# Decoder layer on one core: reloads of the turned x spread over one step, and one copy turned into a maximum

## The reference

```
x = x + self_attention(layernorm(x))      # 32 query heads, 16 key/value heads of 32, causal softmax
x = x + cross_attention(layernorm(x))     # 64 context positions per batch, 8 key/value heads
x = x + ffn(layernorm(x))                 # Wd @ (silu(Wg x) * (Wu x)), 3584 wide, 4-bit weights
```

## Time and profile before

| | |
|---|---|
| median of 3 runs | 2796.19 us (2792.77 to 2798.71) |
| profiled execution, its own time | 2796.21 us |
| its span in the profile | 2794.3 us |
| PE busy | 2581.9 us, 92% of the span |
| DVE busy | 2054.9 us, 74% |
| ACT busy | 1572.4 us, 56% |
| POOL busy | 1235.5 us, 44% |
| DMA, mean | 73 GB/s |

### The profile page before, as it was taken

The page is one execution under the profiler, slowest core; times in us unless marked ns, Lnnn a source line. Parts: engine busy times, 40 slices in busy tenths (PEclk is TensorE's granted clock), DMA queues, the critical chain, the costliest instruction groups (busy, mean ns, idle before and its releaser), DMA issues.

```text
span 2794.3 us, 52658 instructions
## 1 busy us (share of the span) xinstructions
PE 2581.9 (92%) x18536; PEld 1397.0 (50%) x18536; DVE 2054.9 (74%) x2844; ACT 1572.4 (56%) x2794; POOL 1235.5 (44%) x1068
## 2 busy tenths in 40 slices
PE   5889999999974359899999999999999999999999
PEld 3567767667663234344444444444444444444444
DVE  4656768767775768787787869788787868778773
ACT  3456666656663468474655647465564747465550
POOL 2356667767774424252433424243433425243330
PEclk9999999999987669999999999999999999999999
DMA  5243433333222321111111112121111212111112
GB/s 192 91 132 100 121 114 120 102 111 100 81 73 59 128 80 56 51 61 38 60 49 50 53 45 60 38 68 38 53 52 45 61 38 66 40 60 46 52 34 120
DMA packets 153268, 205.34 MB, mean 73 GB/s; under 512 B 34160, under 2 KB 85872, under 8 KB 153072
## 3 DMA queue, kind: packets, MB, share of 16 engines
q1 hardware_dynamic: 153072, 202.97, 23.0%
HBM read 157.16 MB, written 44.04 MB: 72 GB/s over the span
## 4 chain that ended last, share of the span: by engine, by line
PE 60%; DVE 2%; issue 1%; ACT 1%; DMA 1%; POOL 0%; SPq 0%; DVEq 0%; ACTq 0%; POOLq 0%
PE f_bank L1501 39%; PE f_down L1521 21%; DVE line L1625 1%; DMA codes<-in_codes 1%; DVE f_stats L1639 0%; DVE fT_l L1652 0%; ACT f_xn L1561 0%; ACT line L1550 0%; ACT fT_h L1569 0%; PE f_down L1483 0%; DVE w L1631 0%; ACT line L1547 0%; DVE h L1661 0%; DVE y L1666 0%; DVE f_mean_var L1642 0%
## 5 line engine op out<-in xcount | busy, mean ns | idle before, releaser
L1625 DVE TENSOR_TENSOR line<-line 128x512 f32<-128x512 f32 x1008 | 919.4, 962 | 46.7 <-issue 30.9
L1550 ACT ACTIVATE line<-codes 128x512 f32<-128x512 int32 x1008 | 591.2, 620 | 382.6 <-DVE line L1625 284.8
L1501 PE MATMUL f_bank<-fT_h,up_h 128*128 128x512 f16 x1792 | 680.2, 380 | 3.7 <-DVE fT_l L1652 2.4
L1501 PE MATMUL f_bank<-fT_l,up_h 128*128 128x512 f16 x1792 | 680.2, 380 | 0.0
L1501 PE MATMUL f_bank<-fT_h,up_l 128*128 128x512 f16 x1792 | 680.2, 380 | 0.0
L532 POOL TENSOR_TENSOR p_l<-p,p_h 128x512 f16<-128x512 f32 x320 | 369.9, 1164 | 243.0 <-ACT p_h L945 242.6
L1666 DVE SCALAR_TENSOR_TENSOR y<-f_down,y 128x1024 f32<-128x1024 f32 x224 | 274.2, 1224 | 190.7 <-PE f_down L1521 190.7
L1431 POOL TENSOR_TENSOR up_l<-w,up_h 128x512 f16<-128x512 f32 x112 | 145.8, 1301 | 529.2 <-ACT up_h L1555 529.2
L1426 POOL TENSOR_TENSOR w<-w,scales 128x512 f32<-128x512 f32 x168 | 263.8, 1570 | 227.7 <-DVE w L1631 227.7
L1115 DVE TENSOR_REDUCE block_max<-bank 128x4 f32<-128x512 f32 x320 | 218.8, 686 | 195.3 <-PE bank L704 193.0
L1521 PE MATMUL f_down<-dn_h,hT_h 128*128 128x512 f16 x896 | 340.6, 380 | 9.0 <-DVE y L1666 9.0
(11 more groups left out here) (157 smaller groups left out, 4245.4 us busy)
## 6 DMA issues: line engine op xcount, KB each, us to landing
codes<-in_codes SPq DMA_DIRECT2D x168, 256.0 KB, 3.0
scales<-in_scales SPq DMA_DIRECT2D x336, 128.0 KB, 2.9
nat_parts<-nat SPq DMA_DIRECT2D x48, 256.0 KB, 2.0
q_rows<-nat_parts SPq DMA_DIRECT2D x96, 128.0 KB, 2.7
x_unit<-in_x SPq DMA_DIRECT2D x64, 128.0 KB, 2.7
x<-x_unit SPq DMA_DIRECT2D x64, 128.0 KB, 2.3
y<-x SPq DMA_DIRECT2D x4, 2048.0 KB, 12.3
out<-y SPq DMA_DIRECT2D x16, 512.0 KB, 2.6
```

The costliest lines, as they stand in the source:

```text
L1501: mm = nc.tensor.matmul(bank[(GATE, UP)[kind] + n % 2][:, :], w[:, chunk, kind, P * c:P * c + P], x[:, c, cols], start=(m == 0), stop=(m = ...
L1550: op = nc.scalar.activation(line[:, m, :], codes[:, slot, :], ACT.Copy, scale=slope, bias=intercept)
L1625: nc.vector.tensor_tensor(line[:, n + 2, :], line[:, n, :], line[:, n + 2, :], ALU.max)\
```

## The change

`load_turned` takes the part's number i and issues one reload. The four calls move from the head of SP's step i = 10 into step i = 9, between that step's other transfers. The waits of each reload are the same as before: `turned_stored`, and then `x_used` for parts 0 to 2 and `proj_done` for part 3. The third of `row_maxima`'s four instructions becomes a reduction by maximum over an axis of length one.

```diff
-            def load_turned(b):
+            def load_turned(b, i):
                 sp.wait_ge(turned_stored, 16 * TURNED_BY[b])
-                for i in range(QT):
-                    if i < QT - 1:
-                        sp.wait_ge(x_used, (QT - 1) * (b - 1) + i + 1)
-                    else:
-                        sp.wait_ge(proj_done, NP * b)
-                    sp.dma_start(xT[:, i, :, :, :]..., dram["xT"][b % 2, i, :, :]).then_inc(turned_loaded[i], 16)
+                if i < QT - 1:
+                    sp.wait_ge(x_used, (QT - 1) * (b - 1) + i + 1)
+                else:
+                    sp.wait_ge(proj_done, NP * b)
+                sp.dma_start(xT[:, i, :, :, :]..., dram["xT"][b % 2, i, :, :]).then_inc(turned_loaded[i], 16)
...
-                if i == 10 and 0 <= b < B - 1:
-                    load_turned(b + 1)
+                reload = i == 9 and 0 <= b < B - 1
...
                 if s % 2 == 0 and 0 <= s < NS:
                     stack_max(s // 2)
+                if reload:
+                    load_turned(b + 1, 0)
                 q = kind_out(s, 0)
                 if q is not None and q % 4 < 3:
                     store_nat(q)
+                if reload:
+                    load_turned(b + 1, 1)
                 if i % 4 == 0 and u < NU:
                     stack_rows(u, 0)
                     stack_rows(u, 1)
                 if i % 4 == 1 and u < NU:
                     stack_rows(u, 2)
+                if reload:
+                    load_turned(b + 1, 2)
                 if i % 4 == 1 and 2 <= u:
                     store_x1(u - 2)
...
                 if crosses and i % 4 == 1:
                     load_x1(b - 1, i // 4)
                 if crosses and i == 4:
                     lay_values(b - 1)
+                if reload:
+                    load_turned(b + 1, 3)
                 if i == 10 and 0 <= b < B:
                     load_context(b)
...
-                nc.vector.tensor_copy(rows[:, :, :, 0], blocks[:, :, 2:4, 0]).then_inc(rows_maxed, 1)
+                nc.vector.reduce_max(rows[:, :, :, 0], blocks[:, :, 2:4, 0:1], AX_X).then_inc(rows_maxed, 1)
```

More of the change, by code:

```diff
@@ L334, in store_turned @@
                     .then_inc(turned_stored, 16)
-            def load_turned(b):
+            def load_turned(b, i):
                 sp.wait_ge(turned_stored, 16 * TURNED_BY[b])
-                for i in range(QT):
-                    if i < QT - 1:
-                        sp.wait_ge(x_used, (QT - 1) * (b - 1) + i + 1)
-                    else:
-                        sp.wait_ge(proj_done, NP * b)
-                    sp.dma_start(xT[:, i, :, :, :].rearrange("p a c n -> p (a c n)"), dram["xT"][b % 2, i, :, :])\
-                        .then_inc(turned_loaded[i], 16)
+                if i < QT - 1:
+                    sp.wait_ge(x_used, (QT - 1) * (b - 1) + i + 1)
+                else:
+                    sp.wait_ge(proj_done, NP * b)
+                sp.dma_start(xT[:, i, :, :, :].rearrange("p a c n -> p (a c n)"), dram["xT"][b % 2, i, :, :])\
+                    .then_inc(turned_loaded[i], 16)
             def unit_cols(x, u):
```

## The result

The changed kernel takes 2782.04 us, the median of 6 runs (2777.21 to 2783.29), against 2795.79 us for the one before; the ratio is 0.9949 with a 95% interval of 0.9936 to 0.9962. It is faster, by 13.8 us where 21 were forecast. The profiled execution took 2782.7 us.

A forecast was written before the change was run, and what follows sets the result against it. PE was taken to set the pace, waiting for reloads at three crossings: 2796.2 - 18.2 - 5.4 + 1.1 + 1.0 + 0.6 - 0.3 = 2775.0 us. The 8-in-10 range was 2769 to 2786 us.

The forecast's parts named there:

- rival A: At the crossings, the wait moves to piece 2 because part 3 comes 3 us late each time; 2784 us, chance 0.17.
- the forecast's own range: Whole kernel: 2771 to 2780 us, from all waits gone and 1 us from the copy to twice the new waits.
- the prediction's own signs: Right: reload waits under 3 us, clock near 1.0, earlier reload issues, short reduction; wrong: piece 2 waits over 1 us, among others.
- What bounds the kernel, and the early parts: PE sets the pace; at three crossings, early parts 0 and 1 remove 18.2 us of reload waits.
- Part 3: At piece 2 of each crossing, part 3 lands slightly late; new waits 1.1 us in all, bounds 0 and 9.
- The low clock: Behind the three crossing waits, PE's low clock goes with the idleness before it; 5.4 us gained.
- The 0.6 us taken for short waits: Behind the short new waits at crossings, clock loss allowed for PE; 0.6 us, bounds 0 and 3.
- The stacked maxima: In step 10, the small transfer lands late behind part 3 and the turned store; 1.0 us lost, bounds 0 and 5.
- rival C: At crossings, small transfers wait behind big reloads; 8.3 us per crossing, 24.9 in all, 2797.5 us, chance 0.03.
- The copy: On DVE, the maximum avoids waiting for POOL; at most 9.0 us of DVE time goes, 0.3 us of it gained.
- B: On DVE, the copies were on PE's path, so their 9.0 us count in full; 2766 us, chance 0.05.
- D: At the crossings, SP reaches part 0's reload no earlier, so the change does nothing; 2796 us, chance 0.02.

The follow-up runs named there:

- e6: The changed kernel with part 0 reloaded behind the projection's store instead of ahead of it; median 21.6 us below the kernel before.
- e1: The changed kernel with the copy put back for the maximum of length one; 2779.7 us, 16.1 us below the kernel before.
- e4: The changed kernel with part 3's reload right behind part 2's, ahead of the stores and the load of x1; 2775.1 us, 22 us below the kernel before.
- e0: The changed kernel again, unedited, beside others on one chip; 2779.0 us, 16.8 us below the kernel before.
- e8: The changed kernel once more, unedited, on another chip; 13.9 us below the kernel before, ratio interval 0.9929 to 0.9957.
- e2: The kernel before with only the copy made a maximum, reloads unmoved; median 2.5 us below the kernel before, ratio 0.9993 with an interval that includes 1.
- e7: The changed kernel with part 3 right behind part 2 and the stacked maxima ahead of the turned store; 2769.4 us, 27.9 us below the kernel before.
- e9: The same kernel as e7, run on the same chip as e8; 2770.0 us, 26.7 us below the kernel before.
- e10: The kernel of e9 with the copy put back for the maximum; 2773.9 us against 2770.0.
- e5: The changed kernel with the stacked maxima issued ahead of the turned store and store_x2 in each step; 24.8 us below the kernel before.
- e3: The changed kernel with parts 2 and 3 reloaded at the head of step 10 again, only parts 0 and 1 early; 2780.8 us.

## Why the prediction was right, and where it was not

The direction, the main mechanism and the range held; the size was 7 us off, and the time is nearer to rival A's 2784 than to the forecast's 2775. That the range held says little between these two, since it had been stretched to 2786 to take A in. The upper end of the forecast's own range, 2780, was also too high for what it is said to be: twice the new waits would be 2775.0 + 2.7 = 2777.7. By the prediction's own signs the reloads' issues and the reduction came as forecast, but the waits fell to 7.2 us and not under 3, two waits at piece 2 were longer than 1 us, and one stretch stayed at the low clock: these are the signs of A.

*What bounds the kernel, and the early parts.* Right. Parts 0 and 1 are issued at 183.5 and 186.2, in the old times (4.8 us more) 188.3 and 191.0 (188.1 and 190.9 were forecast), land 3.5 to 4.0 us later, and all 18.2 us of the old waits at piece 0 are gone, 3 times out of 3.

*Part 3.* This is the step that failed: "So I put part 3 into the place in the queue that part 0 had, plus 0.5 to 1.8 us", with 1.1 us of waits for it. The waits are 7.2, 6.9 and 5.7 us in the three profiles of the changed kernel. Counted from the issue of the projection's store, part 3 went out 1.7, 1.1 and 2.1 us behind part 0's old place, and it took 1.7, 0.3 and 2.5 us longer to land than part 0 had in the same crossing. So the issues lie inside the 0.5 to 1.8 us but for the third, and the second crossing came as forecast; what failed in the other two is above all the time to land, which was taken over from part 0. Behind both stand transfers that were mis-sized. The projection's store landed 3.2 us after its issue in the first crossing,

```profile
nat_parts<-nat SPq DMA_DIRECT2D x1, 256.0 KB, 3.2
```

and 2.7 and 4.0 in the other two, where I had allowed 0.7 us over the 2.1; e6 takes this away and leaves 4.8 us of waits, no less than the changed order had in e1. And part 3 does not inherit part 0's place: in the first crossing four stores of x1 stood directly ahead of both the earlier trace rows, but ahead of those stores part 0 had only the stacking (landing after 4.3 us), and part 3 has part 2, of which the forecast counted the issue and not the 512 KB. It lands 6.0, 5.8 and 6.8 us after its issue where I had 4.3 and 5.5. The last of the four stores in the first crossing now takes 4.4 us to land; of the others that took 2.2 to 2.4 before, each now takes 3.6 to 4.1. I had reasoned that 1 MB less stood ahead of part 3 than before, and not that 0.5 MB more stood ahead of it than had stood ahead of part 0. e4, which changes only that neighbourhood, brings the waits to none, though not by a shorter way to land (5.8 us) but by the issue 2.7 us sooner behind part 2.

*The low clock.* 5.4 us were to go. In the first two crossings they did, 4.0 of them (clock 1.00 in both stretches); in the third, where PE had waited 4.09 us, it stayed, 2.6 us; e0 and e8 had one such stretch each too (0.57 over 4 us). The 0.6 us taken for short waits was thus too small by 2 us, inside its bounds. The forecast made the clock follow from the waits, so this is the same failure once more.

*The stacked maxima.* 1.0 us forecast, 0.8 at the crossings in the first profile, none in e0 and e8, 1.2 in e1; the 2.7 us of step 18 is a wait that e2 has too. Right in size for the change. e4 and e7, which differ in the order of the maxima and the turned store alone, show that this order is the reason where such a wait comes. The most that the small transfers cost at the crossings is e4's 2.9 us in all, where rival C had 5 us for each.

*The copy.* The reading of the copy beside POOL was right: a reduction lasts 150 ns in the place of 720. The Trainium skill's page "SBUF — State Buffer", section "Who interferes with whom", had said that a reduction on this chip never contends with GpSimd; the trace agrees, with 0.15 us beside a subtraction that covers it. That most of the 9.1 us lie beside other work is shown by e1, e2 and the step times. That 0.3 us of them count is too little: the steps without a crossing show 1.2 us (0.7 and 0.5), and the medians differ by 0.7 (e0 and e1), 2.5 (before and e2) and 3.9 us (e9 and e10), all the same way.

*The sum again, with measured terms:* 2796.2 - 18.2 - 5.4 + 7.2 (part 3) + 0.8 (maxima) + 2.6 (clock behind the third crossing) - 1.0 (the maximum) = 2782.2 us, against 2782.7 in the profiled execution. The 4.8 us gained ahead of the first crossing and the 3.7 and 2.3 lost in step 18 and behind step 44 belong to no term of this sum and leave 1.2 us lost; the crossings gave 0.8 us more than the terms for them, so that the close agreement is partly luck.

*The rivals.* A came true in good part: "the wait moves to piece 2", with part 3 2.5, 0.6 and 4.1 us late where it said 3 each. It had its price right within 2 us and got 0.17 of the chance. The argument against it, less data ahead, was the one that should have been checked against the landings of small stores behind a big load, for which a row stood ready. B falls, since e1 without the maximum is as fast. C's 8.3 us per crossing were not reached anywhere. D falls by the timeline.

What stays open: whether more than 1.2 of the 3.9 us of e10 are the copy's, what e5's and e6's edits are worth by themselves, why the same order of transfers gives waits of 4.4 to 7.2 us, and why single executions differ by up to 6.7 us before the first crossing.

## What to carry to other kernels

When an in-order queue holds several loads for one consumer, move all that the next stage needs as a group, and look at what stands directly ahead of the last one: its landing sets the time, and here stores and loads that nobody waited for, 0.5 to 1 MB ahead of the last reload and 0.5 ahead of the maxima, took back 5 to 10 of the 23.6 us that the early ones could give. Put the transfers with a deadline ahead of those without, small ones too: 4 KB of maxima behind a 512 KB store cost up to 1.5 us per crossing. And price a transfer that moves into traffic by the landings of transfers in traffic, not by its old latency.

## What the runs showed of the hardware that I had not expected

The clock does not follow from the length of the wait ahead alone. Two stretches of e0 begin at the end of a wait of 2.90 us (the first) and of 2.16 us (the second):

```profile
379.50:383.50 4.00, 4.00 (x47) 3.51 (x48) 1.04 (x3) 1.11 (x2) 1.79 (x3) 1.00 0.75 197
575.22:579.22 4.00, 4.00 (x31) 2.86 (x32) 1.75 (x5) 0.28 (x1) 2.53 (x3) 0.57 0.57 153
```

The longer one was followed by a granted clock of 1.00, that is 2.4 GHz throughout, and the shorter one by 0.57, 1.2 GHz for most of 4 us. In e3 a wait of 3.20 us was followed by 1.00 and one of 1.83 us by 0.59, each over the next 4 us. So behind a wait of some 2 us nearly as much again was lost in clock (4 x 0.43 = 1.7 us), or nothing.

A 128 KB store of x1 took 2.2 to 2.4 us from issue to landing behind the stacking alone (the first three of the first crossing before), and 4.8 to 5.3 us behind two reloads (e4). An issue on SP's queue lasted 0.3 to 0.7 us in most cases of these timelines and now and then over 1 us: the turned store's took 1.22 at 194.12, and one of the four stores of x1 in e7 2.17.
